# A transformer block on one core: finer waits for scores, for the transfers of P and for v, the reciprocal's multiple on GpSimd, and a retuned order

## The reference

```python
xn = _layernorm(x)
q, k, v = einsum('bim,mhd->bhid', xn, wq / wk / wv)
q, k = rope(q), rope(k)
s = einsum('bhid,bhjd->bhij', q, k) / 128
p = softmax(s - 1e30 * (i < j))          # causal
o = einsum('bhij,bhjd->bhid', p, v)
attn = einsum('bhid,hdm->bim', o, wo)
h = concatenate([xn, -xn])               # 512
h = relu(s0 * (h @ sign(k0))) * 2        # 1024
h = relu(s1 * (h @ sign(k1))) * 2        # 1024
out = x + attn + s2 * (h @ sign(k2))     # 256
```

## Time and profile before

| | us |
|---|---|
| median of three executions | 1774.23 (1773.61 to 1775.03) |
| the profiled execution | 1775.91 |
| its span in the trace | 1774.1 |
| PE busy, share of the span | 1718.2, 97% |
| DVE | 1534.4, 86% |
| ACT | 1267.5, 71% |
| POOL | 925.6, 52% |
| PE idle and waiting for low halves of `qk` (DVE L635) | 14.6, 15 times |
| for the transposing transfer `pt` | 13.5, 19 times |
| for the one of x (`xT`) | 3.5, 3 times |

### The profile page before, as it was taken

How to read it: one execution, slowest core, us unless ns; L and a number is a source line. 1 busy time by engine, 2 the same in 40 slices (tenths; PEclk the granted TensorE clock), 3 DMA queues, 4 the chain that set the end, 5 groups by cost and what they waited for, 6 DMA issues and landing times.

```text
span 1774.1 us, 34030 instructions
## 1 busy us (share of the span) xinstructions
PE 1718.2 (97%) x12720; PEld 1194.3 (67%) x12720; DVE 1534.4 (86%) x3630; ACT 1267.5 (71%) x2717; POOL 925.6 (52%) x952
## 2 busy tenths in 40 slices
PE   6899989999999999999999999999999999999999
PEld 2356757767676676767767677676766767677667
DVE  8899888897988979888897988979889798888985
ACT  6677676776867677677776867768677776777763
POOL 6555545554545555465455555555456454655632
PEclk9999999999999999999999999999999999999999
DMA  5234543344343434334244333433434344433443
GB/s 172 48 54 73 93 69 78 66 79 81 57 96 60 84 66 71 79 67 91 53 85 83 64 81 67 78 76 63 91 60 88 67 66 85 67 86 58 79 74 69
DMA packets 454838, 134.08 MB, mean 76 GB/s; under 512 B 434704, under 2 KB 453648, under 8 KB 454672
## 3 DMA queue, kind: packets, MB, share of 16 engines
q1 hardware_dynamic: 454672, 131.90, 39.9%
HBM read 14.94 MB, written 8.39 MB: 13 GB/s over the span
## 4 chain that ended last, share of the span: by engine, by line
PE 67%; DVE 19%; ACT 5%; DMA 3%; POOL 3%; issue 2%; SPq 0%; DVEq 0%; POOLq 0%; ACTq 0%
PE bank L489 67%; DVE ph L703 3%; DVE p L666 3%; DVE bank L625 3%; DVE bank L617 2%; DVE qk L635 2%; DMA pt<-ph 2%; ACT p L680 2%; DVE rt L841 1%; POOL xT L319 1%; DVE v L543 1%; DMA xT<-rt 1%; POOL tb L621 1%; DVE hb L822 1%; DVE o L543 1%
## 5 line engine op out<-in xcount | busy, mean ns | idle before, releaser
L697 POOL TENSOR_SCALAR ph<-p,ri 128x384 f16<-128x384 f32 (+3 forms) x512 | 313.2, 612 | 453.9 <-DVE rk L687 416.7
L621 POOL TENSOR_TENSOR tb<-tb,sin 128x512 f32<-128x512 f32 x256 | 331.3, 1295 | 245.2 <-ACT tb L613 238.8
L489 PE MATMUL bank<-hb,wa 128*128 128x256 f16 x3360 | 379.9, 273 | 0.3 <-ACT bank L882 0.3
L489 PEld LDWEIGHTS bank<-hb,wa 128*128 128x128 fp8e5 x3360 | 327.9, 98 | 41.8 <-ACT bank L882 0.5
L680 ACT ACTIVATE p<-p,nm,sc 128x512 f32<-128x512 f32 (+3 forms) x512 | 328.6, 645 | 1.6
L703 DVE SCALAR_TENSOR_TENSOR ph<-p,rk,ph 128x512 f16<-128x512 f32 (+3 forms) x512 | 311.4, 616 | 0.7 <-POOL ph L697 0.7
L666 DVE CUSTOM_DVE_ANT_0 p<-bank,mask 128x512 f32<-128x512 f32 (+3 forms) x512 | 228.9, 484 | 49.9 <-PE bank L489 46.8
L489 PE MATMUL bank<-pt,v 128*128 128x256 f16 (+1 forms) x2304 | 233.1, 256 | 15.1 <-DMA pt<-ph 13.5
L489 PE MATMUL bank<-qk 128*128 128x512 f16 (+3 forms) x1536 | 229.9, 299 | 16.0 <-DVE qk L635 14.6
L489 PEld LDWEIGHTS bank<-pt,v 128*128 128x128 f16 x2304 | 202.6, 98 | 43.0 <-DMA pt<-ph 20.2
L489 PEld LDWEIGHTS bank<-qk 128*128 128x128 f16 x1536 | 132.8, 98 | 121.4 <-DVE qk L635 22.4
(11 more groups left out here) (107 smaller groups left out, 2259.2 us busy)
## 6 DMA issues: line engine op xcount, KB each, us to landing
out<-xnat SPq DMA_DIRECT2D x32, 256.0 KB, 2.4
xnat<-in_x SPq DMA_DIRECT2D x15, 512.0 KB, 3.8
pt<-ph SPq DMA_TRANSPOSE x256, 4.3
o<-in_k SPq DMA_DIRECT2D x1, 1024.0 KB, 7.2
v<-in_wq SPq DMA_DIRECT2D x1, 1024.0 KB, 9.2
v<-in_wk SPq DMA_DIRECT2D x1, 1024.0 KB, 10.9
ph<-in_wv SPq DMA_DIRECT2D x1, 1024.0 KB, 13.5
o<-in_wo SPq DMA_DIRECT2D x1, 1024.0 KB, 10.2
```

The source lines that it names most:

```text
L489: self.todo.append(lambda e, stop=False: e.matmul(self.ps[:, cols[0]:cols[1]], lhsT, rhs, start=first, stop=stop, skip_group_check=skip))
L621: done["crossed", n] = pool.put(lambda e: e.tensor_tensor(tb, tb, SIN[:], ALU.mult))
L697: done["P_hi", g, i] = pool.put(lambda e: e.tensor_scalar(part(r, i, HI), v, RI[:, g % 4, i:i + 1], 4096.0, ALU.mult, ALU.mult))
```

## The change

- `scores`: no wait for both low halves ahead of the fill. Each product waits for the halves that it reads: the first of a tile for both high halves, the second (now low q x high k) for the low half of q, the third (high q x low k) for the low half of k.
- `turned`: one transfer for each square, each with its own distance (`turned_0`, `turned`) and its own semaphore; each waits for the two low halves of its own square. `high` and `values` wait for the square that they touch. `values` waits for the tiles of v one by one.
- `rk` is made by POOL, ahead of the high half of tile 3, in place of DVE.
- The tables PLACES, SETUP, FIRST, EARLY, DELAY, HELD and LATE have other values, and `turned_0` is new in three of them.

```diff
-FIRST = ("am0", "l1", "p0", "l1", "qk", "qk", "qk", "am2", "l1", "qk", "p2", "l1", "S", "qk", "S", "l1", "qk", "l1",
-         "v", "v", "v", "v")
+FIRST = ("am0", "l1", "l1", "p0", "qk", "qk", "am2", "qk", "qk", "l1", "p2", "l1", "S", "qk", "S", "l1", "qk", "l1",
+         "l1", "v", "v", "v", "v")
...
-HELD = dict(am=0, p2=23.2, T=30.9, qk=30.5, S=8.2, PV=23.0, v=13.7, l0=25.3, l1=18.3, seg=21.5, l2=18.6, proj=8.7)
+HELD = dict(am=6.4, p2=30.3, T=29.8, qk=31.0, S=8.4, PV=19.2, v=12.8, l0=25.1, l1=6.6, seg=18.3, l2=26.5, proj=8.4)
...
         def scores(g):
             r = g % 2
-            pe.wait(*[need(("qk_lo", 2 * g + w)) for w in range(2)])
...
-                    f.group((at_col, at_col + w),
-                            three(lambda s: QK[:, r, s, i * 128:i * 128 + 128], lambda s: QK[:, r, 2 + s, 0:w]))
+                    for a, c in ((HI, HI), (LO, HI), (HI, LO)):
+                        f.wait(need(("qk_lo" if a == LO else "qk_hi", 2 * g)),
+                               need(("qk_lo" if c == LO else "qk_hi", 2 * g + 1)))
+                        f.mm((at_col, at_col + w), QK[:, r, a, i * 128:i * 128 + 128], QK[:, r, 2 + c, 0:w])
...
-                dve.wait(done["inv", g])
-                done["inv_k", g] = dve.put(lambda e: e.tensor_scalar(RK[:, g % 4, :], RI[:, g % 4, :], 4096.0, None,
-                                                                     ALU.mult))
 
             def high(i):
-                pool.wait(need(("inv_k", g)))
+                pool.wait(need(("inv", g)))
+                if i == 3:
+                    done["inv_k", g] = pool.put(lambda e: e.tensor_scalar(RK[:, g % 4, :], RI[:, g % 4, :], 4096.0, None,
+                                                                          ALU.mult))
...
-                    pool.wait(need(("pt", g - 2)))
+                    pool.wait(need(("pt", g - 2, SQUARE[i][0])))
...
-            def turned():
-                sp.wait(*[need(("P_lo", g, i)) for i in range(4)], need("pad"))
+            def turned(q):
+                sp.wait(*[need(("P_lo", g, i)) for i in SQUARE if SQUARE[i][0] == q], need("pad"))
...
-                for q in range(2):
-                    a, n = SQ_AT[q], 2 * SQ_SIZE[q]
-                    done["pt", g] = sp.dma(lambda e, a=a, n=n: e.dma_start_transpose(
-                        PT[:, r, a // 128:(a + n) // 128, :], PH[:, r, a:a + n]), s_pt[r], 32 * (g // 2) + 16 * q + 16)
+                a, n = SQ_AT[q], 2 * SQ_SIZE[q]
+                done["pt", g, q] = sp.dma(lambda e: e.dma_start_transpose(
+                    PT[:, r, a // 128:(a + n) // 128, :], PH[:, r, a:a + n]), s_pt[r][q], 16 * (g // 2) + 16)
...
-            at(delay("turned", g), turned)
+            at(delay("turned_0", g), lambda: turned(0))
+            at(delay("turned", g), lambda: turned(1))
...
         def values(g):
             b, h = divmod(g, H)
-            pe.wait(need(("pt", g)))
-            pe.wait(*[need(("vp", b, h // 4, t, LO)) for t in range(4)])
             f = Fill(("PV", g))
             for j, q, i0, i1 in PV_RUNS:
                 keys = 4 if q == 0 else 2
                 base = SQ_AT[q] // 128
+                f.wait(need(("pt", g, q)), need(("vp", b, h // 4, j, LO)))
```

More of the change, by code:

```diff
@@ L70 @@
     "v0_1": ((-4, 4), (-3, 5), (-2, 3), (-2, 2)),
[1 row of a table removed]
[1 row of a table added]
     "v1": ((3, 5), (4, 1), (4, 0), (1, 4)),
[1 row of a table removed]
-    "seg": ((2, 2), (2, 3), (3, 2), (3, 3), (3, 3), (4, 0), (4, 2), (5, 4)),
[1 row of a table added]
+    "seg": ((2, 2), (2, 3), (3, 2), (3, 2), (3, 3), (4, 0), (4, 2), (5, 4)),
     "seg_15": ((2, 0), (3, 4), (4, 1), (4, 2), (5, 2), (5, 4), (5, 5), (6, 5)),
@@ L77 @@
     "l2": ((6, 3), (8, 3)),
-    "l2_15": ((8, 2), (7, 0)),
-    "proj": ((9, 0), (9, 3)),
-}
-SETUP = dict(v_max=96.7, o_max=51.6, a11=46.8, a12=45.5, a22=71.6, s1a=1.2, s1b=18.9, s2a=4.8, s2b=11.7, s3a=4.9,
-             s3b=1.6, s4a=73.7, s4b=89.9, k2=59.9, x1=129.6, wq1=87.8, wk1=113.9, wq2=87.4, wk2=120.1, wq3=107.7,
-             wk3=131.5, wv0=120, wv1=92.1, pads=108.1, ascale=156.1, wo0=146.2, wo1=152.5)
-FIRST = ("am0", "l1", "p0", "l1", "qk", "qk", "qk", "am2", "l1", "qk", "p2", "l1", "S", "qk", "S", "l1", "qk", "l1",
-         "v", "v", "v", "v")
@@ L90 @@
-EARLY = dict(qhi=(23.8, 21.1, 24.7), qlo=(22.9, 20.4, 17.8), bias=(6.3, 7.5, 7.4), exp=(7.3, 2.6, 5.3),
-             inv=(14.5, 0, 10.9), high=(2.7, 14.3, 15.5), low=(20.6, 36.1, 24.1), turned=(42.8, 23.7, 43.6),
-             rotated=(13.8, 15.3, 11.9))
-LAST = ((-1, range(0, 5)), (0, range(5, 7)), (1, range(7, 8)))
-DELAY = dict(hi=0, lo=11.3, swap=0, straight=9.6, crossed=0, rotated=15.5, qhi=21.8, qhi_w=0, qlo=19.8, bias=8.1,
-             exp=11.6, exp_i=1.4, differ=4.7, keep_hi=0, keep_lo=17.4, t_hi=10.6, t_lo=18.1, add=7, inv=23.5,
-             high=22.6, high_i=6.1, low=43.7, low_i=8.3, turned=66.6, x_hi=48.8, x_lo=60.5, x_turned=70.7)
@@ L101 @@
-HELD = dict(am=0, p2=23.2, T=30.9, qk=30.5, S=8.2, PV=23.0, v=13.7, l0=25.3, l1=18.3, seg=21.5, l2=18.6, proj=8.7)
-LATE = dict(rotated=14.1, qhi=19.3, qlo=22.0, bias=4.9, exp=11.3, inv=19.6, high=36.1, low=33.0, turned=46.4)
+    "l2_15": ((8, 1), (7, 0)),
+    "proj": ((9, 0), (9, 2)),
+}
+SETUP = dict(v_max=90.4, o_max=50.7, a11=53.6, a12=40.1, a22=62.5, s1a=0, s1b=13.6, s2a=3.5, s2b=23.2, s3a=0.6,
+             s3b=2.2, s4a=73.1, s4b=89.1, k2=59.3, x1=130, wq1=88.1, wk1=110.9, wq2=86.4, wk2=126.5, wq3=107.7,
+             wk3=131, wv0=119.4, wv1=96.7, pads=105.1, ascale=151.9, wo0=153.3, wo1=150.6)
@@ new lines @@
+FIRST = ("am0", "l1", "l1", "p0", "qk", "qk", "am2", "qk", "qk", "l1", "p2", "l1", "S", "qk", "S", "l1", "qk", "l1",
+         "l1", "v", "v", "v", "v")
+EARLY = dict(qhi=(23.8, 21.1, 24.7), qlo=(22.9, 20.4, 17.8), bias=(6.3, 9.2, 8.4), exp=(6.5, 2.6, 8.5),
+             inv=(11.7, 0, 10.8), high=(0.4, 14.3, 16.5), low=(17.2, 36.1, 29.9), turned=(42.8, 24.6, 44.1),
+             rotated=(13.3, 15.6, 11.9), turned_0=(33.7, 41.4, 36.5))
+LAST = ((-1, range(0, 5)), (0, range(5, 7)), (1, range(7, 8)))
@@ new lines @@
+DELAY = dict(hi=0, lo=10.7, swap=1.7, straight=9.6, crossed=0, rotated=15.5, qhi=21.9, qhi_w=0, qlo=20.4, bias=8.1,
+             exp=11.6, exp_i=1.4, differ=5.3, keep_hi=0, keep_lo=17, t_hi=8.6, t_lo=18.1, add=7, inv=23.5, high=22.2,
+             high_i=4.9, low=43.9, low_i=8.3, turned=70.2, turned_0=61.9, x_hi=46.9, x_lo=60.3, x_turned=71.7)
+HELD = dict(am=6.4, p2=30.3, T=29.8, qk=31.0, S=8.4, PV=19.2, v=12.8, l0=25.1, l1=6.6, seg=18.3, l2=26.5, proj=8.4)
+LATE = dict(turned_0=52.5, rotated=14.7, qhi=22.2, qlo=25.9, bias=4.5, exp=10.3, inv=24.7, high=36.1, low=34.7,
+            turned=46.5)
@@ L223, in block_kernel @@
         s_first = sem("s_first")
-        s_pt = [sem("s_pt0"), sem("s_pt1")]
+        s_pt = [[sem(f"s_pt{r}{q}") for q in range(2)] for r in range(2)]
         s_out = [[sem(f"s_out{i}{f}") for f in range(2)] for i in range(2)]
@@ L700, in low @@
             def low(i):
-                dve.wait(need(("P_hi", g, i)))
+                dve.wait(need(("P_hi", g, i)), done["inv_k", g])
                 v = P[:, r, S_OFF[i]:S_OFF[i] + WIDTH[i]]
```

## The result

The changed kernel takes 1784.97 us (median of four, 1784.08 to 1787.6), the kernel before 1774.63 beside it: a ratio of 1.0062, 95% interval 1.0047 to 1.0076. It is slower by 10.3 us, where 13.4 less was forecast.

What follows compares the result with a forecast made beforehand. PE's matmul columns were the floor, so only its waits, largely set by DVE, could change. Steady part -9.0, 92 to 250 -6.5, tail -1.2, start +3.3 sum to -13.4: median 1760.8 from 1774.23, range 1754.4 to 1771.0.

Steps and rivals of the forecast that it cites:

- Scores two products ahead: Steady part, scores: two products run before the wait for k's low half, winning 0.43 per element; 0.84 stays.
- rival A: Steady scores: bank comes free too late for two products ahead; only `rk`'s 0.20 per element is won, 1767.0; chance 0.12.
- `rk`: Steady part: moving this multiply to GpSimd costs 0.27 there and wins DVE 0.20 per element before the scores.
- GpSimd's idle time elsewhere covers the delay: GpSimd outside the examined head: idle before such a group, 5.45 in the row, covers delay from `rk`.
- The transfers: P's transfers to PV: issuing the large square 1.9 sooner removes the `pt` waits, 0.53 each in the steady part.
- 92 to 250: Stretch before the steady part: `pt` waits and half-clock loss total 7.5; 6.5 won, as DVE may take some back.
- The start: Start of kernel: new order costs +3.3 (0 to +8); scores 0 at 55.3, scores 3 1.5 late.
- The tail: End of kernel: one `pt` wait of 1.04 idle goes, winning 1.2 by starts.
- Late next is DVE, which is counted already: Steady part, after `pt` waits go: DVE is the next limit, already included in the 0.64 won per element.
- Rival C: Start: eight weight-split low halves meet GpSimd, 2.29 each for 0.74; start costs 19.3, total about 1780; chance 0.09.
- The estimate from the Trainium skill: `rk` on GpSimd: twice its 0.17 on DVE, 0.34 in place of 0.27; the 9.0 won would stay.

Runs made afterwards that it cites:

- the edits alone: Finer scores waits, one transfer per square and `rk` on GpSimd, with the tables of the kernel before: 1762.26, ratio 0.9929 to the kernel before.
- One swap: Changed kernel with keep_lo 17 put back to 17.4, so tile 2's P low half precedes two first-layer low halves on DVE: 1765.76.
- four tries: Against the 1762.26 kernel: first-layer fills earlier 1794.56; v fill and P lows moved 1799.59; P lows later alone 1779.10; P lows earlier, one low half later 1775.78.

## Why the prediction was wrong

**Scores two products ahead: right.** Expected 0.43 per element and 0.84 left; measured 0.43 (1.27 against 0.84), and 0.73 left at the scores in the edits alone, 0.74 with the new tables. Where it is lost depends on the tables: with the new ones 0.55 of it stands before the third product, as forecast; with the old ones 0.58 stands before the first, for the bank that the low half of v reads. So rival A's late bank is there too, but it holds the two products back by a part only.

**`rk`: the size right, the gain not.** It takes 0.23 (mean of 128; 0.27 forecast) on GpSimd and 0.20 is won on DVE in that stretch. What failed is the clause that GpSimd's idle time elsewhere covers the delay. It covers GpSimd's own queue, but not DVE, whose low halves are held by what stands behind `rk` there and is now 0.3 later: 0.32 more at one of them (0.94 for 0.62).

**The transfers: waits right, gain nothing.** The `pt` waits went as forecast in the steady part; per square or paired makes no difference there. In 92 to 250 the 3.46 wait shrank to 0.5, but the scores behind it took it back. I took 6.5 of 7.5 as gained, since "DVE may take some back"; with paired transfers the whole kernel is as fast.

**The start: the rows close, the sum by luck.** Scores 0 were forecast at 55.3; the rows have 54.89. The wait for Wq has 3.67 for 4.8 and that for `p2` 5.06 for 6.0:

```profile
32.90 2.33 PE L490 MATMUL bank<-xT,wq 128*128 128x512 f16 x6 [3.67 <-DVE wq L366]
...
48.68 0.59 PE L490 MATMUL bank<-dg,p 128*128 128x2 f32 x2 [5.06 <-DVE dg L346]
49.13 5.06 PE L490 MATMUL bank<-hb 128*128 128x512 f16 x12
54.03 1.03 PE L490 MATMUL bank<-hb,rt 128*128 128x512 f16 x4
54.89 1.79 PE L490 MATMUL bank<-qk 128*128 128x512 f16 x12
```

Scores 3 end at 92.1 here for 93.1 before, 1.0 sooner where 1.5 later was forecast. In four other kernels with the new start they end at 93.0 to 95.9, in eight with the old one at 92.6 to 94.5; the means, with these two, are 94.2 and 93.3, so the new start costs 0.9, within the spread. At the scores of head 5, by which the forecast had lost its 3.3, the changed kernel is 1.0 behind (118.28 for 117.24). At the end of the scores at 257 it is 3.3 ahead, and the sum had 3.2 (+3.3 - 6.5); but it got there by 1.0 - 4.3. Two terms were each over 2 us too large, and that they cancel is luck. The tail won 1.9 where 1.2 was forecast.

**The step that failed: "Late next is DVE, which is counted already."** It was counted to the scores and no further. 22 us behind them DVE had 0.56 to spare at a bank, which no step looked at: the 0.43 that the scores win alone nearly uses it up (0.11 is lost there in the edits alone). And the durations of its low halves were taken to stay. The reordering that spoiled them is one instruction of the built order, low half of tile 2 behind two first-layer low halves, and stands in no step of the prediction; of DVE's moves I had named only those next to the scores. The term left out is 14 x 1.585 = +22.2. With it, -13.4 + 22.2 = +8.8, and the span grew by 8.2. Rival C had the sign, but at another place: weight splits in the start, which meet GpSimd in the same way. Of the eight of Wq and Wk one does (1.76 for 0.75). The rows of the forecast itself (2.29 for a split beside a POOL operation, 0.74 alone) held the effect; I asked it of the start alone.

**The estimate from the Trainium skill** (GPSIMD Engine Reference, Key points: VectorE about 2x faster for elementwise work) was 0.34 for `rk`; the trace has 0.23 against 0.17. It spoke against the move, and the move wins nothing, though for another reason than speed.

**What holds the low halves**, as the rows show it: a low half of P, with both inputs in SBUF, that comes behind one of the long GpSimd operations, a rotary product or a high half of P waits until that one ends (2.24 and 1.26 beside 2.13 and 1.16); an instruction with an input in PSUM does not (0.41). What is left of it behind the end of GpSimd's goes by its own columns: 0.28 for 256, 0.41 for 384, 0.55 for 512. Not every GpSimd instruction holds it: a low half of 256 columns that starts 0.42 behind the 128x4 power of 1.04 takes 0.47, as alone, in all 13 places. Beside the norm's 128x256 instructions in the start, too, low halves end before GpSimd's does. DVE and POOL of after:

```profile
862.27 0.47 DVE L705 SCALAR_TENSOR_TENSOR ph<-p,rk,ph 128x256 f16<-128x256 f32 x1
...
861.85 1.04 POOL L310 TENSOR_TENSOR rs<-ve,half 128x4 f32<-128x4 f32 x1 [1.78 <-DVE ve L308]
```

POOL is held by DVE too: the second of its two halves came while a low half ran, and the pair took 2.58 for 2 x 1.16. The Trainium skill (SBUF - State Buffer, section SBUF: two separate sides) states this rule: the two engines share a pair of SBUF ports, which whichever starts first keeps for its whole instruction, and a DVE instruction with two SBUF inputs is among those that need it. The trace agrees, but for the 128x4 power and the norm's instructions, which read SBUF too. The prediction did not weigh that page; by it, a swap that puts a low half of P behind a POOL instruction can cost up to the length of that instruction. Here 1.62 came beside 2.13.

## What to carry to other kernels

Where one engine is busy for nearly all of a stretch (here 18.53 of 18.73 us), a shorter wait of another engine inside it was worth nothing, and a longer instruction on the busy one was paid, less what was to spare, at the next place where something waited for it: follow its chain to that place, and ask how much is to spare there. When a schedule is retuned, compare durations of the same instruction before and after, not only the order: busy time that stays equal though instructions went is the sign. And try to put the instructions that read SBUF alone beside short GpSimd ones, those that read PSUM beside the long ones; one number of a table did 19 us here. Follow the low halves behind the moved one too, since over half of what DVE won there came from one that no edit touched.

## What the runs showed of the hardware

- A DVE low half of P (both inputs in SBUF) that starts behind one of GpSimd's long operations, rotary products or high halves of P ends behind that one's end, by 0.41 for 384 columns (2.24 for 0.62 beside 2.13, 1.26 beside 1.16) and 0.55 for 512 (1.69 for 0.74 beside 1.27). One that reads a bank lasts as ever (0.41; 105 such in one trace).
- A GpSimd instruction on 128x4 did not hold it: 0.47 beside the power of 1.04, in 13 of 13. Why is not shown.
- The hold is by the instruction. Two GpSimd instructions of half the size in place of one took 18 us off the kernel (one run), though GpSimd needs longer for them (2.58 for 2.13).
- A 4-column multiply takes 0.23 on GpSimd, 0.17 on DVE.
- Moving a low half out of one meeting can bring another in: in three of four tries a low half was held again, the same one (2.1), one of the next head (2.08) and, in the last, three within 10 us. One swap (1765.76) went the other way and undid two.
